# Shuffle transfers begun in two groups of eight, and a weighing lag of five steps, in the L0 cross-attention of a two-layer perceiver block

## The reference, cut to what matters

```python
# L0 cross-attention: 16 heads of 64, context x2 of 2 x 2048 rows of 128
q = x1 @ Wq
k, v = split(x2 @ Wkv)
attn = softmax(einsum('bhid,bhjd->bhij', q, k) * 64 ** -0.5)
out  = einsum('bhij,bhjd->bhid', attn, v) -> (b, l, 1024)
return out @ Wo + bo
```

## Time and profile before

| | us |
|---|---|
| median of 3 executions | 459.5 (459.15 to 459.7) |
| the profiled execution | 458.62 |
| its span | 456.8 |
| PE busy | 410.4 (90% of the span) |
| DVE busy | 336.6 (74%) |
| ACT busy | 271.2 (59%) |
| POOL busy | 232.9 (51%) |

### The profile page before, as it was taken

One profiled execution on the slowest core, in us unless ns is written; L12 is line 12 of the kernel. 1 busy time (PEld: TensorE's weight loads), 2 busy tenths in 40 slices (PEclk: granted clock), 3 DMA queues, 4 the chain that ended last, 5 costly groups with the idle time before them and its releaser, 6 DMA issues.

```text
span 456.8 us, 8194 instructions
## 1 busy us (share of the span) xinstructions
PE 410.4 (90%) x3214; PEld 336.0 (74%) x3214; DVE 336.6 (74%) x498; ACT 271.2 (59%) x398; POOL 232.9 (51%) x138
## 2 busy tenths in 40 slices
PE   7996998999999999998898886999879999976896
PEld 6764787997978988887897453674657788854695
DVE  5798888897988899884224946804689999954664
ACT  4466758777677767667433363410169999962244
POOL 0022996987789978688730474100055664510024
PEclk9998899999999999999999997999999999998999
DMA  7728687768886776877971000699970000010000
GB/s 232 285 65 186 136 186 168 181 154 202 230 196 154 174 179 141 200 158 176 395 294 52 0 1 1 128 214 207 196 286 3 3 2 4 1 33 0 0 2 11
DMA packets 18645, 59.80 MB, mean 131 GB/s; under 512 B 5808, under 2 KB 7600, under 8 KB 16944
## 3 DMA queue, kind: packets, MB, share of 16 engines
q1 hardware_dynamic: 18608, 59.30, 50.9%
HBM read 19.30 MB, written 0.13 MB: 43 GB/s over the span
## 4 chain that ended last, share of the span: by engine, by line
PE 40%; DVE 16%; SPq 14%; issue 8%; POOL 7%; ACT 7%; DMA 7%; POOLq 0%; ACTq 0%; DVEq 0%
SPq L480 8%; POOL dT_lo L1268 6%; SPq L511 6%; PE ps L613 4%; DMA kstack<-k_lo 4%; PE ps L968 3%; PE ps L615 3%; PE ps L614 3%; PE ps L874 3%; PE ps L895 3%; DVE w_ring L1541 3%; PE ps L591 3%; PE ps L592 3%; PE ps L593 3%; DVE max L1393 3%
## 5 line engine op out<-in xcount | busy, mean ns | idle before, releaser
L1268 POOL TENSOR_TENSOR dT_lo<-z_sq,dT_hi 128x1024 fp32r<-128x1024 f32 x60 | 142.3, 2398 | 27.0 <-ACT dT_hi L997 26.9
L1063 ACT ACTIVATE y_sq<-ps,nmax 128x1024 f32<-128x1024 f32 x64 | 70.8, 1112 | 49.8 <-DMA z_sq<-y_sq 27.7
L1393 DVE TENSOR_REDUCE max<-ps 128x1 f32<-128x1024 f32 x64 | 77.7, 1214 | 18.5 <-PE ps L593 18.4
L613 PE MATMUL ps<-dT_hi,ctx_hi 128*128 128x256 f32 x256 | 74.9, 293 | 5.8 <-POOL dT_lo L1268 5.4
L1383 DVE STREAM_TRANSPOSE y_sq<-y_sq 128x1024 f32<-128x1024 f32 x60 | 74.1, 1234 | 2.3 <-ACT y_sq L1063 2.3
L615 PE MATMUL ps<-dT_hi,ctx_lo 128*128 128x256 f32 x256 | 72.3, 282 | 0.0
L614 PE MATMUL ps<-dT_lo,ctx_hi 128*128 128x256 f32 x256 | 72.3, 282 | 0.0
L1541 DVE SCALAR_TENSOR_TENSOR w_ring<-ps,neg_nbias,cap 128x1024 f32<-128x1024 f32 x56 | 67.6, 1276 | 3.6 <-PE ps L874 3.6
L1202 ACT ACTIVATE p_ring<-w_ring,nbias_sb 128x1024 f32<-128x1024 f32 x56 | 62.2, 1146 | 1.5 <-DVE w_ring L1541 0.8
L997 ACT ACTIVATE dT_hi<-z_sq 128x1024 fp32r<-128x1024 f32 x60 | 60.7, 1059 | 3.7 <-DMA z_sq<-y_sq 2.2
L591 PE MATMUL ps<-ctxT_hi,qk_hi 128*128 128x512 f32 x128 | 54.0, 422 | 7.7 <-ACT y_sq L1063 7.5
(11 more groups left out here) (209 smaller groups left out, 651.1 us busy)
## 6 DMA issues: line engine op xcount, KB each, us to landing
z_sq<-y_sq SPq DMA_DIRECT2D x240, 128.0 KB, 2.4
w_sb<-in_w SPq DMA_DIRECT2D x2, 2048.0 KB, 16.3
kstack<-k_hi SPq DMA_DIRECT2D x8, 512.0 KB, 11.1
kstack<-k_lo SPq DMA_DIRECT2D x8, 512.0 KB, 12.5
ctx_raw<-in_ctx_nat SPq DMA_DIRECT2D x2, 1024.0 KB, 8.4
ctxT_raw<-in_ctx_t SPq DMA_DIRECT2D x1, 2048.0 KB, 9.6
wg_sb<-in_wg SPq DMA_DIRECT2D x1, 1088.0 KB, 14.2
wu_sb<-in_wu SPq DMA_DIRECT2D x1, 1088.0 KB, 16.5
```

Source lines behind the costliest of these rows:

```text
L613: mm(acc, hi[:, k, :], dT_hi[m % 3][:, cols], start=(k == 0), stop=False)
L1063: nc.scalar.activation(out_t, keys, ACT.Exp, bias=nmax[:, hs % 2:hs % 2 + 1], scale=SCALE0, accum_out=rowsum[:, hs, p:p + 1]).then_inc(exp ...
L1268: nc.gpsimd.tensor_tensor(d_ring(dT_lo, m), z_chunk(m), d_ring(dT_hi, m), ALU.subtract).then_inc(d_lo, 1)
L1393: return v.tensor_reduce(max2[:, 2 * (hs % 2) + p:2 * (hs % 2) + p + 1], slot(2 * hs + p), AX.XY, ALU.max)
```

## The change

The keys are dealt to the squares by score chunk: group c of y_sq now holds the 512 keys of score chunk c, so half p of a step fills groups 2p and 2p + 1. The transfers of groups 0 and 1 (eight) need the first halves of both steps only and wait for `squared >= 4 * pr + 3`; the eight others wait for 4 * pr + 4. Each eight has its own semaphore. The context rows are loaded in the matching order, in four transfers instead of one. LAG is 5 instead of 6. The low parts of m = 53, 55, 57 and 59 are made on DVE, in its steps 30 to 33, instead of on POOL. The order of turns and weighs behind the last scores is new, and turn waits for all exponentials. copy_o adds the two half sums of a row by two tensor_scalars with one number per partition each, instead of one tensor_tensor of two columns.

```diff
-        spread = (sem("spread0"), sem("spread1"))
+        d_lo_dve = sem("d_lo_dve")
+        spread = [[sem(f"spread{i}_{p}") for p in range(2)] for i in range(2)]
+        def rest(engine, m):
+            return engine.tensor_tensor(d_ring(dT_lo, m), z_chunk(m), d_ring(dT_hi, m), ALU.subtract)
+        def rest_done(m):
+            on_dve = sum(k <= m for k in ON_DVE)
+            return (d_lo_dve, on_dve) if m in ON_DVE else (d_lo, m + 1 - on_dve)
         def y_half(hs, p):
-            return y_sq[:, hs // 2 % 2, :, hs % 2, GRP // 2 * p:GRP // 2 * (p + 1)]
+            return y_sq[:, hs // 2 % 2, 2 * p:2 * p + 2, hs % 2, :]
         def z_chunk(m):
-            return z_sq[m // 4 % 3][:].rearrange("p a h (d t i) -> p d t (a h) i", d=4, t=4)[:, m % 4]
+            return z_sq[m // 4 % 3][:].rearrange("p a h (t d i) -> p d t (a h) i", d=4, t=4)[:, m % 4]
-        LAG = 6
+        LAG = 5
+        ON_DVE = (53, 55, 57, 59)
+            def get_rows(b, raw_t, s):
+                for c in range(4):
+                    rows = ins["ctx_nat"][:, b * NBLK + 4 * c:b * NBLK + 4 * c + 4, :]
+                    get(raw_t[32 * c:32 * c + 32, :].rearrange("i (k n) -> i k n", k=4), None, s,
+                        rows.rearrange("(k i) u d -> i k (u d)", k=4))
-            get(ctx_raw0[:], "ctx_nat", "ctx0", ins["ctx_nat"][:, 0:NBLK, :].rearrange("p k d -> p (k d)"))
+            get_rows(0, ctx_raw0, "ctx0")
             for pr in range(NPR - 1):
-                sp.wait_ge(squared, 4 * pr + 4)
+                sp.wait_ge(squared, 4 * pr + 3)
                 for c in range(4):
+                    if c == 2:
+                        sp.wait_ge(squared, 4 * pr + 4)
                     for a in range(4):
                         sp.dma_start(z_sq[pr % 3][32 * c:32 * c + 32, a, :, :],
-                                     y_sq[32 * a:32 * a + 32, pr % 2, c, :, :]).then_inc(spread[pr % 2], 16)
+                                     y_sq[32 * a:32 * a + 32, pr % 2, c, :, :]).then_inc(spread[pr % 2][c // 2], 16)
                 if m < ND:
-                    pe.wait_ge(d_lo, m + 1)
+                    pe.wait_ge(*rest_done(m))
             def turn(m):
-                pe.wait_ge(exped, 2 * NHS - 1 + d // 2)
+                pe.wait_ge(exped, 2 * NHS)
             weigh(m)
             turn(ND)
-            project_v(NPR - 4)
             weigh(m + 1)
             weigh(m + 2)
             turn(ND + 1)
+            project_v(NPR - 3)
             weigh(m + 3)
+            turn(ND + 2)
             weigh(m + 4)
-            turn(ND + 2)
-            project_v(NPR - 3)
             weigh(m + 5)
-            weigh(m + 6)
-            weigh(m + 7)
             turn(ND + 3)
             def d_round(m):
-                act.wait_ge(spread[pr % 2], 256 * (pr // 2 + 1))
+                for p in range(2):
+                    act.wait_ge(spread[pr % 2][p], 128 * (pr // 2 + 1))
             def exp_half(hs, p):
-                if p == 0 and hs % 2 == 0 and pr >= 2:
-                    act.wait_ge(spread[pr % 2], 256 * (pr // 2))
+                if hs % 2 == 0 and pr >= 2:
+                    act.wait_ge(spread[pr % 2][p], 128 * (pr // 2))
             for m in range(ND):
+                if m in ON_DVE:
+                    continue
                 pool.wait_ge(d_hi, m + 1)
             def copy_o(pr):
-                link(v.tensor_tensor(r, rowsum[:, 2 * pr:2 * pr + 2, 0], rowsum[:, 2 * pr:2 * pr + 2, 1], ALU.add))
+                for j in range(2):
+                    halves = rowsum[:, 2 * pr + j, :]
+                    s = v.tensor_scalar(r[:, j:j + 1], halves[:, 0:1], halves[:, 1:2], None, ALU.add)
+                link(s)
                 for m in (2 * (w + 1), 2 * (w + 1) + 1):
-                    if ND <= m < NCH:
+                    if m in ON_DVE:
+                        dve.wait_ge(d_hi, m + 1)
+                        rest(v, m).then_inc(d_lo_dve, 1)
+                    elif ND <= m < NCH:
                         e_rest(m)
```

More of the change, by code:

```diff
@@ L478, in _ @@
                 for c in range(4):
+                    if c == 2:
+                        sp.wait_ge(squared, 4 * pr + 4)
                     for a in range(4):
                         sp.dma_start(z_sq[pr % 3][32 * c:32 * c + 32, a, :, :],
-                                     y_sq[32 * a:32 * a + 32, pr % 2, c, :, :]).then_inc(spread[pr % 2], 16)
+                                     y_sq[32 * a:32 * a + 32, pr % 2, c, :, :]).then_inc(spread[pr % 2][c // 2], 16)
                 if pr == 6:
                     sp.wait_ge(scored, 2 * H)
-                    get(ctx_raw1[:], "ctx_nat", "ctx1", ins["ctx_nat"][:, NBLK:, :].rearrange("p k d -> p (k d)"))
-            sp.wait_ge(spread[0], 256 * (NPR // 2))
+                    get_rows(1, ctx_raw1, "ctx1")
+            for p in range(2):
+                sp.wait_ge(spread[0][p], 128 * (NPR // 2))
             get(wo0[:], "wo0", "o0")
-            sp.wait_ge(d_lo, ND - 4)
+            sp.wait_ge(*rest_done(ND - 6))
+            sp.wait_ge(*rest_done(ND - 5))
             get(ctxT_raw2[:], "ctx_t", "ctxT2")
@@ L626, in turn @@
                     for j in range(2):
-                        at = j * CTX + (4 * d + t) * P
+                        at = j * CTX + (4 * t + d) * P
                         last = nc.tensor.transpose(
@@ L1016, in split_n @@
                 hi_t, _, src = ctx_part(b, g)
-                act.wait_ge(load["ctx" + str(b)], 16)
+                act.wait_ge(load["ctx" + str(b)], 64)
                 copy(hi_t, src).then_inc(split_hi, 1)
@@ L1053, in exp_half @@
                 act.wait_ge(maxed, hs + 1)
-                if p == 0 and hs % 2 == 0 and pr >= 2:
-                    act.wait_ge(spread[pr % 2], 256 * (pr // 2))
[L1056 to L1062, removed]
+                if hs % 2 == 0 and pr >= 2:
+                    act.wait_ge(spread[pr % 2][p], 128 * (pr // 2))
+                out_t, keys = y_half(hs, p), slot(2 * hs + p)
+                if pr == NPR - 1:
+                    out_t = y_sq[:, pr % 2, :, :, :].rearrange("p c h n -> p (c h n)")
+                    out_t = out_t[:, hs % 2 * CTX:(hs % 2 + 1) * CTX].rearrange("p (k c i) -> p c k i", k=NBLK, c=4)
+                    out_t, keys = out_t[:, 2 * p:2 * p + 2], keys.rearrange("p c (k i) -> p c k i", k=NBLK)
                 nc.scalar.activation(out_t, keys, ACT.Exp, bias=nmax[:, hs % 2:hs % 2 + 1], scale=SCALE0,
@@ L1266, in _ @@
             for m in range(ND):
+                if m in ON_DVE:
+                    continue
                 pool.wait_ge(d_hi, m + 1)
-                nc.gpsimd.tensor_tensor(d_ring(dT_lo, m), z_chunk(m), d_ring(dT_hi, m), ALU.subtract).then_inc(d_lo, 1)
+                rest(nc.gpsimd, m).then_inc(d_lo, 1)
                 step = m // 2 + LAG - 1
@@ L1278, in _ @@
             pool.wait_ge(turned, 4)
-            pool.wait_ge(d_lo, ND)
+            pool.wait_ge(*rest_done(ND - 2))
             nc.gpsimd.memset(vx[:, :, :, DC:DC + 1], 1.0)
```

## The result

| | before | changed |
|---|---|---|
| median of 4 executions side by side | 459.6 us (459.15 to 461.41) | 474.15 us (470.97 to 475.77) |
| ratio, with its 95% interval | | 1.028 (1.0244 to 1.0316) |
| profiled execution, span | 458.62, 456.8 | 473.67, 471.9 |
| end of the L0 cross-attention | 241.57 | 255.70 |

A forecast was written before the change was run, and what follows sets the result against it. It took TensorE, busy 90% of the span, as the bound. Ramp +6.6, steady part +0.9 and tail -0.4 made +7.1 us on the profiled 458.62, so 465.7; against the median, 466.6 us, range 459 to 472.5.

The forecast's parts named there:

- account of a pair: Steady part: weigh 0.8 us late plus 0.4 from slow issues, halved, so a pair loses 0.6 us, as before (0.59).
- Ramp, term 1: Start of L0 cross-attention: d_rounds queued ahead of step 4's exponentials delay weigh(0), plus half clock; +6.6 us, bounds 4.2 and 7.4.
- Steady part, term 2: L0 cross-attention's pairs: low parts cost what exponentials no longer do; +0.9 us, bounds -5.9 and +4.
- Edits at nothing: Context rows in four loads and new key order: no cost charged; pair 7 may leave 0.6 us late (0.3 after halving).
- Tail, term 3: End of L0 cross-attention: TensorE waits 3.5 us against 3.3 and some 0.6 before; -0.4 us, bounds -3.1 and +1.
- third rival: copy_o's row sum still queues behind POOL: ten pairs at 0.6 us more, 472 to 473 us; chance 0.06.
- first rival: Early transfers free TensorE, if 0.8 us is missing from the steady chain: faster, 457.2 us; chance 0.15.
- The fourth: Rival: the second eight transfers hold the queue, landings no sooner, 1.5 us more per pair, 481 us; chance 0.03.

The follow-up runs named there:

- run 4: The kernel before with copy_o's row sums made by two tensor_scalars: 460.25 us, ratio 0.9989.
- run 6: The changed kernel with all low parts on POOL, none on DVE: 474.55 us, ratio 1.0293.
- run 5: The changed kernel (LAG 5) with a pair's first eight transfers also waiting for both halves of its second step: 501.75 us, ratio 1.0871.
- Run 2: The changed kernel with ACT's d_round(0) and d_round(1) moved behind the exponentials of step 4 and the fourth split: 469.77 us, ratio 1.0226.
- run 9: The changed kernel with fifteen products of zeros on TensorE ahead of weigh(0): 472.27 us, ratio 1.0229.
- run 3: The changed kernel without the 1 MB load of batch 1's context rows (batch 1's results wrong): 469.57 us, ratio 1.0227.
- run 7: The changed kernel with six products of zeros on TensorE ahead of weigh(0): 475.11 us, ratio 1.0277.
- run 8: The changed kernel with LAG 6, POOL making dT_lo(0), dT_lo(1) earlier and xb later, batch 1's load in two halves, its splits later: 450.12 us, ratio 0.9755.
- run 10: The changed kernel with copy_o's row sums by one tensor_tensor again: 480.37 us, ratio 1.0387.
- run 11: The changed kernel with LAG 6 and POOL's new order only (dT_lo(0), dT_lo(1) earlier, xb later), load whole: 447.38 us, ratio 0.9702.
- run 1: The changed kernel with LAG 6 and the tail order of before: 450.36 us, ratio 0.9802.

## Why the prediction was right or wrong, point by point

**Direction, and the step of lag against the earlier transfers: right.** The medians of four kernels put the two halves of the change side by side:

| | sixteen at once | eight and eight |
|---|---|---|
| lag 6 | 459.6 | 450.36 |
| lag 5 | 501.75 | 474.15 |

(The kernel at the upper left differs from the one at its right in more than the transfers, the row sum and the four low parts on DVE among it; runs 4 and 6 show these at nothing, the first at lag six, the second at lag five. The order of loads and keys was not taken apart.) Earlier transfers gain 9 us; the shorter lag, whose cover they were meant to pay for, costs 24. In the steady part the first transfer of a pair leaves 4.0 us behind the first scores of the step in which its last halves are turned, and 7.06 in run 5: 3.1 us sooner, where a step of lag is 5.86. What the change gives is less than what it takes. The prediction's account of a pair says the same.

**Ramp, term 1: right in every step.** Forecast and measured: landing 39.1 and 39.7; the exponential 43.75 and 44.39, of which 0.6 is the later landing (issues from 27.07 to 37.32 took 10.25 us and not 9.68); weigh(0) 51.4 and 51.85; weigh(8) 77.8 and 78.59. Of the cost, weigh(8) stands 4.02 us later and two halves (2.8) behind: 6.8 us, forecast 6.6. Run 2 shows the chain, run 9 the clock's share in it, 1.9 for an estimated 2.4.

**Steady part, term 2: right in its sum, apart from pair 7.** No wait for exponentials is left. In run 3, without the load, the ten pairs from weigh(8) to weigh(48) take 12.33 us each, and 12.26 in before; the forecast had them at 12.32. With bounds of -5.9 and +4 around the term, so near a hit is in part luck. The term by its own numbers (6.6 against 5.9) is +0.7 and not the +0.9 that was added up; measured to weigh(50) it is +0.7. The shape was half right: of the pairs 2 to 12 three, six, eight and eleven have no wait at their first weigh, pair 7 has 4.74, and the six others wait 0.51 to 1.69 us (the largest just behind the ramp). That this stretch keeps its time although TensorE's cover shrank by a step is what the account of a pair, (0.8 + 0.4) / 2 us lost, said.

**The step that failed is in "Edits at nothing".** The four loads of context rows were charged as three more issues, "pair 7 may leave 0.6 late (0.3 after halving)". The issues were priced, the bytes weren't. The load moved from a place with a gap of 3 us behind it to one with 0.4, because pair 7's transfers now leave sooner; and a stretch of sixteen transfers, at a DMA share of about 0.9 by itself, has little spare bandwidth in which to catch up. The measured term is 5.6 us (weigh(56) with and without the load, run 3), of which 4.0 is waiting and most of the rest half clock. The sum made again for the profiled executions: 6.8 in the ramp, 0.7 in the steady part, 5.6 at pair 7, -0.7 in the tail without its half clock and 1.6 for that half clock, 14.0; L0's end moved by 14.13. The last 1.6 us were in no term either. They stand in the trace of the changed kernel and in none of runs 2, 3, 6, 7 and 9, and what decides it is open. The medians make the load cheaper: 4.6 us.

A reading of before points to it: the DMA share beside the load, 0.94 at 114 to 118 us, was not read, although the prediction itself moved the transfers' start by 3.1 us towards the load. (The 4.1 us of the earlier trace rows would not have: it is the last transfer of pair 13, issued at 199.48, far from the load.) That packets of rows a quarter as long move slower can't be told from this: the load of before ran at 286 GB/s with transfers around it, the new one at 209 to 216, but among other transfers. A smaller or otherwise cut load at lag five was not tried; run 8, with it in halves, lost pair 7's wait at lag six.

**Tail, term 3: the sum of its waits right, its shares not, its clock missing.** 3.5 us of waits, as forecast; but the 0.9 and 2.6 ahead of the turn and weigh(56) came as 0.6 and 1.8, and the wait ahead of weigh(52), forecast at 0.4 and not counted, took 1.1. A rest on DVE took 2.24 and 2.54 us for m = 53 and 57, with POOL at a low part of its own, and 1.22 for m = 55 and 59, with POOL idle (bounds 1.2 and 3.6). No wait of TensorE was ended by one of them.

**copy_o and the third rival.** The row sum takes 0.2 us in all 32 cases, so the third rival did not come. Run 10 has the old form at lag five: 480.37, 6.2 us more. That equals the rival's 10 pairs at 0.6 by luck, since 4.4 of it fall at pair 10. The rule of the Trainium skill (SBUF — State Buffer, section "Who interferes with whom"), that a DVE instruction with two inputs in SBUF contends with a GpSimd instruction reading SBUF, fits both: the tensor_tensor of 256 numbers took up to 2.34 us in run 10, and each of those over 0.35 us ended 0.02 us behind a low part of POOL; the tensor_scalars never took over 0.21, in the midst of such low parts too.

**The first rival** (faster, 457.2) was right about the transfers and wrong about the lag: at lag six they bring 450.4. Its condition, 0.8 us missing from the chain, did not come true. **The fourth** (second eight hold the queue) is refuted by run 5: with all sixteen waiting for the fourth square the time is 27.6 us more. In the trace of the changed kernel the ninth issue follows the eighth by 0.64 us in pairs 3 to 14; the second eight stand back in pair 1 (3.1 us) and pair 2 (1.7) only.

**The range.** It took in the bounds of the three terms but none for the load, which had been set at nothing by an argument on issues. The wait of 4.74 us also brought half clock; the prediction had charged that in the ramp alone.

## What to carry to other kernels

A transfer that starts sooner hides the same number of microseconds, not a pipeline step: compare the two before giving a step of lag away, and try the first without the second. When transfers run back to back, read their DMA share: here they took 0.9 of the DMA engines alone, and a load of 1 MB put in front still delayed all the transfers of the next pair and, less, those of the pair after it. Price such a load by its bytes and not by its issues. And price a new TensorE wait of a few microseconds twice, once for the wait and once for the clock that may fall behind it.

## What was not expected of the hardware

- The clock fell again 3.4 us after it had come back. In run 7 it was at half for 3.4 us from 43.6 and full from 47.0 to 50.4, though TensorE stood still for the 4.28 us ahead of 51.78, and then at half for 6.8 us just as weigh(0) was near. Nearly the same gap can do either: 2.05 us (run 11) left it full, 2.06 (run 8) was followed by half clock through 48 to 51 us; 3.20 (run 9, ahead of the products) left it full, 3.24 (run 1) did not.
- Waits of 3.7 to 5.2 us in the midst of a busy stretch were met by half clock too, for 3.4 or 6.8 us (run 5, and pair 7). In the tail of the changed kernel 3.4 us of half clock followed a wait of 1.78 us; a wait of 1.58 at the same place in run 3 was not followed by any. So the distance from 461 to 502 us is more than the sum of the waits.
- POOL and DVE lengthen each other's low parts: POOL's of m = 58 took 3.37 us beside the DVE's of m = 57 at 2.54, where POOL's mean is 2.41 and the DVE's take 1.22 with POOL idle.

```profile
229.35 5.67 POOL L386 TENSOR_TENSOR dT_lo<-z_sq,dT_hi 128x1024 fp32r<-128x1024 f32 x2 [4.55 <-ACT dT_hi L1016]
```

```profile
230.25 2.54 DVE L386 TENSOR_TENSOR dT_lo<-z_sq,dT_hi 128x1024 fp32r<-128x1024 f32 x1 [3.18 <-ACT dT_hi L1016]
```
